# Layer 1 of a four-layer attention kernel: small clamps and scalings go to VectorE

## The reference

```python
def _fq(x, delta, zp, n_bits):
    xi = _round_ste(x / delta) + zp
    xq = jnp.clip(xi, 0.0, 2.0 ** n_bits - 1.0)
    return (xq - zp) * delta

def _attn(x, ctx, wq, wk, wv, wo, bo, dq, dk, dv, dw):
    ...
    sim = jnp.einsum('bhid,bhjd->bhij', _fq(q, dq, 128.0, 8), _fq(k, dk, 128.0, 8)) * SCALE
    attn = jax.nn.softmax(sim, axis=-1)
    out = jnp.einsum('bhij,bhjd->bhid', _fq(attn, dw, 0.0, 8), _fq(v, dv, 128.0, 8))
    ...
```

## Time and profile before

| | |
|---|---|
| median of 3 runs | 5165.88 us (5164.52 to 5167.72) |
| profiled execution, its own time | 5168.09 us |
| its span, first to last instruction | 5166.3 us |
| mean granted TensorE clock, share of full speed | 0.971 |
| busy over the span: PE, DVE, ACT, POOL | 94%, 57%, 55%, 42% |
| layer 1 by its GpSimd work (L1735) | 985.4 to 2319.0 us |

### The profile page before, as it was taken

How to read it: one execution, slowest core, us unless ns; L and a number is a source line. 1 busy time by engine, 2 the same in 40 slices (tenths; PEclk the granted TensorE clock), 3 DMA queues, 4 the chain that set the end, 5 groups by cost and what they waited for, 6 DMA issues and landing times.

```text
span 5166.3 us, 91631 instructions
## 1 busy us (share of the span) xinstructions
PE 4838.5 (94%) x34496; PEld 3541.4 (69%) x34496; DVE 2968.7 (57%) x6704; ACT 2851.6 (55%) x9051; POOL 2148.0 (42%) x4307
## 2 busy tenths in 40 slices
PE   8999999968787787889999999999999999999998
PEld 5666666656666665666666666666667778877777
DVE  5555555556566656664455445544555676767765
ACT  4555555677888888873333333233333566666664
POOL 2333333477877778771111111111112444444443
PEclk9999999989898988999999999999999999999999
DMA  2000000010000000001000000000001100000000
GB/s 79 20 20 20 22 21 20 17 40 17 14 20 11 20 17 14 17 30 38 13 11 13 14 13 10 13 12 12 13 10 31 35 18 21 18 17 21 18 17 10
DMA packets 40039, 103.09 MB, mean 20 GB/s; under 512 B 4912, under 2 KB 21552, under 8 KB 38192
## 3 DMA queue, kind: packets, MB, share of 16 engines
q1 hardware_dynamic: 39600, 97.23, 6.0%
HBM read 82.53 MB, written 14.68 MB: 19 GB/s over the span
## 4 chain that ended last, share of the span: by engine, by line
PE 80%; ACT 9%; POOL 7%; DVE 2%; issue 2%; DMA 0%; SPq 0%; ACTq 0%; DVEq 0%
PE ring L1268 47%; PE ring L1219 12%; PE score L1200 11%; ACT e L1378 5%; POOL e L1735 4%; PE ring L1250 3%; PE ring L1243 3%; POOL e L1745 2%; PE ring L1257 2%; PE ring L1216 1%; DVE nmax L1513 1%; POOL rsumw L1728 1%; POOL work L1721 1%; ACT probs L1418 1%; PE score L1195 1%
## 5 line engine op out<-in xcount | busy, mean ns | idle before, releaser
L1738 POOL TENSOR_SCALAR e<-e,rsum 112x375 f32<-112x375 f32 (+1 forms) x2048 | 1103.3, 556 | 2678.9 <-DVE rsum L1520 2676.7
L1378 ACT ACTIVATE e<-score,nmax 112x375 f32<-112x375 f32 (+1 forms) x2048 | 1042.5, 536 | 384.9 <-DVE nmax L1513 381.0
L1513 DVE TENSOR_REDUCE nmax<-score 112x2 f32<-112x750 f32 (+1 forms) x1152 | 1079.7, 953 | 301.1 <-PE score L1200 299.8
L1418 ACT COPY probs<-ring 125x336 f32<-125x336 f32 (+1 forms) x976 | 403.8, 448 | 1318.7 <-PE ring L1219 1256.9
L1268 PE MATMUL ring<-h,weights 128*128 128x224 f32 x3840 | 910.0, 370 | 5.8 <-ACT h L1350 2.7
L1219 PEld LDWEIGHTS ring<-consts,e 112*125 112x125 f32 x4608 | 590.7, 188 | 272.3 <-issue 138.6
L1200 PE MATMUL score<-keys,q 64*112 64x375 f32 (+2 forms) x3584 | 619.9, 503 | 162.9 <-ACT e L1378 150.5
L1268 PEld LDWEIGHTS ring<-h,weights 128*128 128x128 f32 x3840 | 707.8, 197 | 89.9 <-issue 24.9
L1219 PE MATMUL ring<-consts,e 112*125 112x112 f32 x4608 | 675.1, 281 | 6.7 <-DVE heads L1604 4.3
L1378 ACT ACTIVATE e<-score,nmaxc,quant 112x375 f32<-112x375 f32 (+1 forms) x1024 | 555.2, 554 | 10.7
L1268 PE MATMUL ring<-weights,ctx 128*125 128x256 f32 (+1 forms) x1536 | 560.6, 495 | 0.1
(11 more groups left out here) (121 smaller groups left out, 5844.4 us busy)
## 6 DMA issues: line engine op xcount, KB each, us to landing
ctx<-ctx_t SPq DMA_DIRECT2D x128, 375.0 KB, 3.0
out_t<-x SPq DMA_DIRECT2D x64, 224.0 KB, 1.9
x<-out_t SPq DMA_DIRECT2D x48, 224.0 KB, 2.5
weights<-weights SPq DMA_DIRECT2D x7, 1024.0 KB, 5.2
x<-x_t SPq DMA_DIRECT2D x16, 224.0 KB, 2.5
weights<-weights SPq DMA_DIRECT2D x1, 3328.0 KB, 10.7
weights<-weights SPq DMA_DIRECT2D x1, 2304.0 KB, 9.1
weights<-weights SPq DMA_DIRECT2D x1, 2048.0 KB, 7.3
```

The source lines that it names most:

```text
L1378: ins = nc.scalar.activation(e_of(u)[:, n * width:(n + 1) * width], score_bank(u)[0:S, n * width:(n + 1) * width], ACT.Exp, bias=minus, sc ...
L1418: ins = nc.scalar.copy(dst, src)
L1513: ins = dve.tensor_reduce(to, src, AX, ALU.max, negate=True)
L1738: ins = nc.gpsimd.tensor_scalar(mine, mine, rsum[0:S, slot(u), n:n + 1], 0.0, ALU.mult, ALU.add)
```

## The change

Three steps of layer 1 change their engine, and the planner's costs are changed with them. The clamp of a quantised product is made by VectorE with the same operands. The scaling of the maximum is made by VectorE right behind the maximum (a wait on `shifted` between them), and `maxed` is signalled by the scaling. The scaling of the reciprocal is made by VectorE right behind the reciprocal (a wait on `ranked` between them), and `inverted` is signalled by it. The DMAs, the tiles and the number of arithmetic instructions stay. Since `arrange` works with the costs and engines, each engine's order can come out differently.

```diff
     def save_cost(self, j):
         if j.kind == "turn":
-            return 0.5
+            return 0.38 if j.layer == 1 else 0.5
...
-            self.add("max", p, "V", 1.12 if own else 0.96, p.index + 0.3)
-            self.add("exp", p, "A", (2.9 if own else 1.3) + (0.3 if q else 0), p.index + 0.5)
-            self.add("invert", p, "V", 0.17, p.index + 0.9)
-            self.add("weigh", p, "G", (2.7 if own else 1.15) + ((1.4 if own else 1.3) if q else 0), p.index + 1.0)
+            self.add("max", p, "V", (1.12 if own else 0.96) + (0.3 if q else 0), p.index + 0.3)
+            self.add("exp", p, "A", 2.9 if own else 1.3, p.index + 0.5)
+            self.add("invert", p, "V", 0.42 if q else 0.17, p.index + 0.9)
+            self.add("weigh", p, "G", (2.7 if own else 1.15) + ((1.1 if own else 1.0) if q else 0), p.index + 1.0)
...
-                self.add("clamp", j, "G", 0.55 if j.kind in ("ck", "cv") else 0.4, j.pos + 0.3)
+                self.add("clamp", j, "V", 0.55 if j.kind in ("ck", "cv") else 0.35, j.pos + 0.3)
...
@@ scalar_exp
-            if o.layer == 1:
-                nc.scalar.activation(nmaxc[0:S, pair_slots(p), 0:count_of(o)], nmax[0:S, pair_slots(p), 0:count_of(o)],
-                                     ACT.Identity, scale=quant[0:S, a + 4:a + 5]).then_inc(shifted, 1)
-                wait.wait_ge(shifted, eight_bit_nth(p, "exp"))
...
@@ vector_program
                     ins = dve.tensor_reduce(to, src, AX, ALU.max, negate=True)
+                    if o.layer == 1:
+                        a = 0 if is_own(o) else 8
+                        ins.then_inc(shifted, 1)
+                        wait.wait_ge(shifted, eight_bit_nth(p, "max"))
+                        ins = dve.tensor_scalar(nmaxc[0:S, pair_slots(p), 0:nt], to, quant[0:S, a + 4:a + 5], None, ALU.mult)
                     ins.then_inc(maxed, 1)
...
                     ins = dve.reciprocal(to, sums[0:S, pair_slots(p), 0:nt])
+                    if o.layer == 1:
+                        a = 0 if is_own(o) else 8
+                        ins.then_inc(ranked, 1)
+                        wait.wait_ge(ranked, eight_bit_nth(p, "invert"))
+                        ins = dve.tensor_scalar(rsumw[0:S, pair_slots(p), 0:nt], to, quant[0:S, a + 3:a + 4], None, ALU.mult)
                     ins.then_inc(inverted, 1)
...
+                elif kind == "clamp":
+                    rows, width = quantised_shape(x_)
+                    r = rounded[0:rows, x_.place % 4, 0:width]
+                    wait.saves([x_])
+                    dve.tensor_scalar(r, r, ROUND + 127.0, ROUND - 128.0, ALU.min, ALU.max).then_inc(clamped, 1)
...
@@ pool_program
-                if kind == "clamp":
-                    rows, width = quantised_shape(x_)
-                    r = rounded[0:rows, x_.place % 4, 0:width]
-                    wait.saves([x_])
-                    nc.gpsimd.tensor_scalar(r, r, ROUND + 127.0, ROUND - 128.0, ALU.min, ALU.max).then_inc(clamped, 1)
-                    continue
...
-                if o.layer == 1:
-                    a = 0 if is_own(o) else 8
-                    nc.gpsimd.tensor_scalar(rsumw[0:S, pair_slots(p), 0:count_of(o)], rsum[0:S, pair_slots(p), 0:count_of(o)],
-                                            quant[0:S, a + 3:a + 4], 0.0, ALU.mult, ALU.add).then_inc(ranked, 1)
-                    wait.wait_ge(ranked, eight_bit_nth(p, "weigh"))
```

More of the change, by code:

```diff
@@ L1100, in four_layers @@
         eight_bit = {}
-        for kind, by in (("exp", "A"), ("weigh", "G")):
+        for kind, by in (("max", "V"), ("invert", "V"), ("weigh", "G")):
             ps = [x_ for k_, x_ in plan.order[by] if k_ == kind and x_.octet.layer == 1]
```

## The result

The changed kernel takes 5209.16 us (median of 4 runs, 5207.74 to 5210.49) where the kernel before takes 5165.2: a ratio of 1.0084, 95% interval 1.0067 to 1.0102. It is 44 us slower. The forecast was 5106, and the range to 5172 does not hold it.

A forecast was written before the change was run, and what follows sets the result against it. Layer 1 was bound by a chain changing engines, none full. Per period 6.9 us removed less 1.9 returned gave 5.0, four fifths 4.0; times 15 streams, 60 us off: 5106 us, forecast 5070 to 5130, range 5045 to 5172.

The forecast's parts named there:

- 10.0 + 5.1 = 15.1: Layer 1, work added on VectorE per period: 40 scalings at 0.25 us make 10.0 us, 16 clamps make 5.1 us.
- (2.2 + 1.2 + 0.8 in pauses - 0.75 put back) x 0.8 x 15: Layer 1's chain, scalings: us per period for rsumw, nmaxc and pauses, less VectorE's return; four fifths kept, 15 streams.
- rival 4: Layer 1: the planner's new order could be worse by chance, 2 us per period, 30 us, giving 5136 us; chance 0.10.
- the last sentence of the prediction: Layer 1: the prediction would be most wrong if order, not load, holds the layer together; no size given.
- (2.2 + 0.5 - 1.1) x 0.8 x 15: Layer 1's chain, clamps: us per period removed, their pauses, less VectorE's return; four fifths kept, 15 streams.
- Rival 1: Layer 1: clamps on VectorE hold GpSimd 5.1 us per period, leaving no gain, 5166 us; 0.08 including otherwise hidden changes.
- Rival 2: Layer 1: VectorE becomes the bound, clamp waits delaying maxima and evictions; 2.5 us per period longer, 5204 us; chance 0.15.
- its sign: Layer 1: ScalarE and TensorE wait more for VectorE's maxima and evictions, with long VectorE waits before clamps; no size given.
- Rival 3: Layer 1: all 6.9 us per period go and some clock returns (sign: granted 0.93 or more), 5050 us; chance 0.12.
- 16 x 0.04 us: Layer 1: meeting GpSimd costs the 16 clamps on VectorE 0.04 us each, 0.6 us per period.

The follow-up runs named there:

- m2: Kernel before with only the planner's cost of layer 1's turn changed from 0.50 to 0.49, all work on its old engines: 5190.39 us, ratio 1.0043.
- e3: Changed kernel's order of steps, but all three moved steps made by their old engines: 5333.55 us, ratio 1.0324 to the kernel before.
- e4: Kernel before with only the clamps moved to VectorE, steps kept in the order planned with old costs and engines: 5167.51 us, ratio 1.0002.
- the order of 0.38: Order planned with old costs except layer 1's turn at 0.38, not 0.50: 5183.92 us without moves, 5128.57 with both scalings, 5158.52 with all three moves.
- e1: Kernel before with both scalings moved to VectorE, clamps left on GpSimd, order planned with old costs and engines: 5135.84 us, ratio 0.994.
- e2: Kernel before with all three moves made, order from old costs, clamps put into VectorE's list by planned time: 5155.25 us, ratio 0.9979.

## Why the prediction was wrong

**Right: what bounds layer 1, and the loads.** A path through all engines sets the period, GpSimd's weighing lost its share of the chain, and DVE's 64.5 us per period came out as 64.2. Layer 0 was untouched. That DVE's figure is so close is partly luck. The durations of the scalings and clamps add up to 154.5 / 13 + 74.4 / 13 = 17.6 us per period where the prediction had 10.0 + 5.1 = 15.1. But VectorE's instructions overlap their neighbours (in the trace of the changed kernel a scaling of 0.23 us starts at 1736.52 and the next instruction at 1736.66), so its busy time rose by 14.8 us only; and the planner moved 20 of its 179 clips in 13 periods to ScalarE.

**Right in kind: the scalings.** By the terms of the prediction they were worth (2.2 + 1.2 + 0.8 in pauses - 0.75 put back) x 0.8 x 15 = 41 us; the three orders measured 31, 55 and 65.

**The step that failed: rival 4, "the new order spoils half", was sized at 30 us off a gain and could only shrink it.** In the sum itself a change of order stood at nothing. The forecast of 60 us off and the 44 us on lie 104 apart, and the order is about half of it, 54 us; it is also what turned a gain of 12 us into a loss. I had read that every list comes out anew and treated it as a small disturbance, while a hundredth in one cost is worth 23 us here (m2). With 17 to 32 us of idle time per period on each engine, the order of steps decides how much of it there is, at nearly the same load; the last sentence of the prediction named this and gave it no chance of its own. The old order was the best of those measured without moves, four with e3's. The two kernels that cured one of its longest waits gained nothing, so this step is not the cause; that the loss is spread over many places is likely and not shown. Which property makes an order good stays open, and so does whether the new costs are bad by chance or by rule.

**The other half: the moves with the order held.** They gave 12 us where 60 had been worked out. The scalings fell 10 us short in the old order (31 for 41), and the clamps, counted as a gain of (2.2 + 0.5 - 1.1) x 0.8 x 15 = 19 us, cost 19 behind the scalings: 38 us, the larger error of the two.

**Failed: the clamps.** Alone they change nothing (e4), and behind the scalings they cost 19 to 35 us. The prediction added up pieces that stood on one chain. In the old order the scalings take GpSimd's weighing out of the head of the chain and put VectorE's nmax, nmaxc, probs and rsumw there, so that VectorE's added work can show. This is not the whole cause: alone, with GpSimd still on the chain (13.3% weighing), the clamps gained nothing either, and in the order of 0.38 the chain of the kernel with both scalings still has GpSimd's weighing at 10.1%, and the clamps cost 30 us. The windows over 1150 to 2150 us show the loads, first without the clamps (e1), then with them (e2), in the old order:

```profile
1150.00:2150.00 1000.00, 810.42 (x6626) 668.46 (x6624) 746.49 (x2127) 783.40 (x2262) 736.99 (x1503) 0.92 0.06 17
```

```profile
1150.00:2150.00 1000.00, 811.07 (x6458) 670.69 (x6459) 783.10 (x2271) 761.96 (x2218) 637.76 (x1272) 0.90 0.05 16
```

VectorE goes from 74.6 to 78.3% busy and GpSimd from 73.7 to 63.8%. TensorE's wait with the value products for a transposed tile that VectorE moves grows between the two, 20.9 us in 12 waits to 30.9 (L1257 and L1266 are the same line):

```profile
PE ring L1257 <- DVE probs L1587: 20.9, 12, 1.8
```

```profile
PE ring L1266 <- DVE probs L1601: 30.9, 12, 2.7
```

**Rival 1**, clamps that hold GpSimd for their own length, 5.1 us per period, did not come. Its sign was a longer L1735. Here are the means before and after:

```profile
L1735 POOL TENSOR_SCALAR e<-e,rsumw 112x375 f32<-112x375 f32 x416 | 241.8, 594 | 20.4
L1735 POOL TENSOR_SCALAR e<-e,rsumw 112x375 f32<-112x375 f32 x416 | 252.5, 617 | 294.5 <-DVE rsumw L1526 294.2
```

That is 23 ns more on 32 instructions, 0.7 us per period, and the line's other form, 112x112, went from 413 to 408 ns.

**Rival 2** named the right total, 5204 against 5209, mostly for a wrong reason. In the old order a VectorE with all three moves is 12 us faster than before, and the wait in front of clamps is 22.1 us in 26 waits, not 62. Part of its sign came true all the same: ScalarE waits longer for maxima (80.0 to 99.3 us), and once the scalings are moved, bringing the clamps to VectorE costs 19 to 35 us.

**Rival 3's** sign did not come: the granted clock of layer 1 is 0.86, not 0.93. The range also leaves out a little more than the prediction allowed itself: 0.15 + 0.12 / 2 = 0.21.

**Undersized: meeting GpSimd.** Line by line over the changed kernel's steady stretch, min/median/max in ns:

```profile
L1514 DVE TENSOR_SCALAR nmaxc<-nmax,quant x259: 227/231/590, 1151.4 to 2250.1; 112x2 f32<-112x2 f32 x104, 112x8 f32<-112x8 f32 x26
L1526 DVE TENSOR_SCALAR rsumw<-rsum,quant x260: 227/229/570, 1153.6 to 2256.9; 112x2 f32<-112x2 f32 x104, 112x8 f32<-112x8 f32 x26
L1553 DVE TENSOR_SCALAR work<-work x209: 276/297/589, 1153.8 to 2254.8; 128x224 f32<-128x224 f32 x52, 128x375 f32<-128x375 f32 x26, 125x256 f32<-125x256 f32 x14, 112x256 f32<-112x256 f32 x13
L1745 POOL TENSOR_SCALAR e<-e x520: 517/522/1327, 1151.3 to 2257.3; 112x375 bf16<-112x375 f32 x139, 112x448 bf16<-112x448 f32 x35
```

The medians are near the minima, except for the clamps' mixed widths, and the prediction judged by a median. The means by form lie well above:

```profile
L1514 DVE TENSOR_SCALAR nmaxc<-nmax,quant 112x2 f32<-112x2 f32 x207 | 69.9, 338 | 7.3
L1526 DVE TENSOR_SCALAR rsumw<-rsum,quant 112x2 f32<-112x2 f32 x208 | 53.0, 255 | 7.4
L1553 DVE TENSOR_SCALAR work<-work 128x224 f32<-128x224 f32 x78 | 28.3, 362 | 25.0 <-ACT work L1435 22.1
```

A scaling of a maximum, 227 ns at least, takes 338 on average, some 110 ns more, and it stands between a maximum and the exponentials. The clamp of 224 columns takes 362 where 277 was counted, and GpSimd's longest L1745 went from 662 to 1327 ns (while its longest L1735 fell from 1672 to 1296). The timelines of both engines show two cases:

```profile
1749.11 1.10 POOL L1745 TENSOR_SCALAR e<-e 112x448 bf16<-112x448 f32 x2
1749.16 0.54 DVE L1514 TENSOR_SCALAR nmaxc<-nmax,quant 112x2 f32<-112x2 f32 x1
...
1738.86 0.23 DVE L1514 TENSOR_SCALAR nmaxc<-nmax,quant 112x8 f32<-112x8 f32 x1
1741.79 2.72 POOL L1735 TENSOR_SCALAR e<-e,rsumw 112x112 f32<-112x112 f32 x8 [5.44 <-DVE rsumw L1526]
```

The first scaling has GpSimd at work beside it and takes 0.54 us; the second falls into 5.44 us in which GpSimd stands idle and takes 0.23. Counted over the steady stretch of the changed kernel, the 39 two-element scalings of maxima during which GpSimd did nothing took 227 to 231 ns each, and the 169 others 363 on average. For the reciprocals it is 143 at 227 to 230 and 65 at 314 on average, for the clamps of 224 columns 39 at 276 to 278 and 39 at 448. So the extra time comes only beside a working GpSimd.

The Trainium skill (SBUF — State Buffer, Who interferes with whom) has VectorE's two-port instructions and GpSimd exclude each other for a whole instruction. The trace agrees in that time is lost only where the two overlap; the longest scaling, 590 ns, is 363 above the minimum, less than one GpSimd instruction of 517 ns. In which mode so small an instruction runs, no run here shows.

The prediction's "16 x 0.04 us" judged meeting by a median and by the clamps only, and left the 40 scalings out. Still it is no more than a part: over the two-element scalings it is (111 x 16 + 28 x 16) ns, 2.2 us of added durations per period, and the scalings gained 31 to 65 us all the same. Nor is it the order's loss: with all moves in the old order (e2) the durations of scalings and clamps add up to some 17.5 us per period, as much as in the changed kernel (17.6). What of the clamps' loss is meeting and what is VectorE's load was not taken apart.

## What to carry to other kernels

Where a planner writes the order and no engine is full, a change of costs is a change of the kernel: keep the order fixed to judge a move, and draw several orders (a hundredth in one cost was enough here) before an order is judged or kept. Costs nearer to the true work did not give a better order here. Pieces that are removed from one chain don't add up: two scalings gained 9 and 4 us alone and 31 together, and the clamps' 2.2 us of chain were worth nothing alone and less than nothing behind the scalings. Here the version to keep is both scalings on VectorE with the clamps on GpSimd, 5125 to 5136 us.

## What was not expected of the hardware

A two-element instruction on VectorE took 227 to 231 ns whenever GpSimd stood idle, and up to 590 where the two overlapped. For sizes as small as these the mean is the number to plan with, and it depends on how often the instruction falls beside GpSimd's work: 338 ns for the maxima (169 of 208 beside it), 255 for the reciprocals (65 of 208).
